# A four-stage block (two attentions, two feed-forward parts): x and weights split into f16 halves in SBUF and transposed by DMA in place of TensorE

## The reference, cut to what matters

```python
x = x + tanh(g_xattn[0]) * L0_xattn(layernorm(x), ctx, Wq, Wg, bg, Wkv, Wo)     # 16 heads, linear attention, sigmoid gate
x = x + tanh(g_ffn[0])   * L0_ffn(layernorm(x), proj1, b1, proj2, b2)           # 512 -> 2048 -> 512, gelu
x = x + tanh(g_xattn[1]) * L1_xattn(layernorm(x), ctx, mask)                    # softmax over 64 memory tokens
x = x + tanh(g_ffn[1])   * L1_ffn(layernorm(x), gate_w, gate_up, down, ...)     # router, 8 experts of 192, silu(gate) * up
```

## Time and profile before

| | |
|---|---|
| median of 3 runs | 1939.32 us (1937.81 to 1941.26) |
| the profiled execution's own time | 1941.13 us |
| its span, first to last instruction | 1939.3 us |
| TensorE (PE) busy | 1900.6 us, 98% |
| weight loads (PEld) | 962.7 us, 50%, beside PE |
| VectorE (DVE) | 1035.4 us, 53% |
| ScalarE (ACT) | 559.7 us, 29% |
| GpSimd (POOL) | 280.7 us, 14% |
| mean granted TensorE clock | 0.994 |
| DMA | 86.99 MB, mean 45 GB/s |

### The profile page before, as it was taken

The page is one execution under the profiler, slowest core; times in us unless marked ns, Lnnn a source line. Parts: engine busy times, 40 slices in busy tenths (PEclk is TensorE's granted clock), DMA queues, the critical chain, the costliest instruction groups (busy, mean ns, idle before and its releaser), DMA issues.

```text
span 1939.3 us, 25583 instructions
## 1 busy us (share of the span) xinstructions
PE 1900.6 (98%) x10102; PEld 962.7 (50%) x10102; DVE 1035.4 (53%) x2260; ACT 559.7 (29%) x873; POOL 280.7 (14%) x277
## 2 busy tenths in 40 slices
PE   6999998999999999999999999999999999999999
PEld 4556555644444444444444444444544444444444
DVE  7688866764545453443535545554555555545422
ACT  3145423422222221112212233232222333333321
POOL 3023211111102010101100011111111111111111
PEclk9999998999999999999999999999999999999999
DMA  6013322220101111110101020101010101000000
GB/s 218 12 42 124 106 89 82 87 98 17 44 28 60 28 64 50 56 55 22 62 1 55 1 71 1 50 1 50 1 50 1 50 1 45 5 11 13 1 22 22
DMA packets 56041, 86.99 MB, mean 45 GB/s; under 512 B 9042, under 2 KB 17362, under 8 KB 55922
## 3 DMA queue, kind: packets, MB, share of 16 engines
q1 hardware_dynamic: 55922, 85.36, 13.8%
HBM read 60.17 MB, written 25.17 MB: 44 GB/s over the span
## 4 chain that ended last, share of the span: by engine, by line
PE 86%; issue 8%; DVE 3%; POOL 1%; DMA 1%; ACT 1%; POOLq 0%; SPq 0%; DVEq 0%
PE bank L835 44%; PE bank L939 16%; PE bank L1033 10%; PE bank L844 5%; PE bank L919 4%; PE bank L885 1%; PE bank L904 1%; POOL arena L802 1%; PE bank L1020 1%; PE bank L968 1%; PE bank L995 0%; DMA x_after_ffn<-arena 0%; PE bank L984 0%; PE bank L983 0%; DMA arena<-x_after_attention 0%
## 5 line engine op out<-in xcount | busy, mean ns | idle before, releaser
L835 PE MATMUL bank<-arena 128*128 128x512 f16 x4608 | 1043.4, 380 | 3.1 <-DVE arena L1286 2.3
L835 PEld LDWEIGHTS bank<-arena 128*128 128x128 f16 x4608 | 451.0, 98 | 522.7 <-issue 5.5
L939 PE MATMUL bank<-arena 128*128 128x512 f16 x1536 | 352.1, 379 | 1.2 <-DVE arena L1469 1.2
L1033 PE MATMUL bank<-arena 128*128 128x512 f16 x1152 | 264.3, 379 | 0.9 <-POOL arena L802 0.9
L1621 DVE SCALAR_TENSOR_TENSOR arena<-bank,arena 128x512 f32<-128x512 f32 x96 | 72.0, 750 | 332.1 <-PE bank L835 332.1
L939 PEld LDWEIGHTS bank<-arena 128*128 128x128 f16 x1536 | 150.1, 98 | 173.9 <-DVE arena L1469 1.7
L1467 DVE TENSOR_SCALAR arena<-arena 128x512 f16<-128x512 f32 x128 | 69.4, 543 | 305.4 <-ACT arena L1134 305.2
L1134 ACT ACTIVATE arena<-bank,arena 128x512 f32<-128x512 f32 x128 | 99.6, 778 | 457.3 <-PE bank L835 454.3
L802 POOL TENSOR_TENSOR arena<-arena 128x512 f16<-128x512 f32 x96 | 111.1, 1157 | 628.7 <-ACT arena L1171 628.7
L844 PE MATMUL bank<-arena 128*128 128x128 f32 x1012 | 150.1, 279 | 26.4 <-DVE arena L1234 14.1
L1033 PEld LDWEIGHTS bank<-arena 128*128 128x128 f16 x1152 | 112.1, 98 | 128.3 <-POOL arena L802 1.4
(11 more groups left out here) (173 smaller groups left out, 1221.9 us busy)
## 6 DMA issues: line engine op xcount, KB each, us to landing
arena<-in_L_ffn_proj SPq DMA_DIRECT2D x48, 256.0 KB, 2.9
x_after_attention<-arena SPq DMA_DIRECT2D x8, 1024.0 KB, 4.7
arena<-x_after_attention SPq DMA_DIRECT2D x8, 1024.0 KB, 5.6
x_after_ffn<-arena SPq DMA_DIRECT2D x8, 1024.0 KB, 4.5
arena<-x_after_ffn SPq DMA_DIRECT2D x8, 1024.0 KB, 6.2
arena<-in_x SPq DMA_DIRECT2D x7, 1024.0 KB, 5.4
out<-arena SPq DMA_DIRECT2D x7, 1024.0 KB, 4.2
arena<-in_L_ffn_down_proj SPq DMA_DIRECT2D x48, 96.0 KB, 2.0
```

The lines of the kernel that those rows point to most:

```text
L835: m = e.matmul(bank[b][:, :], wT[l][:, c, tile * P:(tile + 1) * P], y[h][:, c, :], start=n == 0, stop=n == NPASS - 1)
L939: m = e.matmul(bank[t][:, :], hv[h][:, 0, t * P:(t + 1) * P], w2T[l][:, j, :], start=j == 0 and i == 0, stop=j == NH - 1 and i == 2)
L1033: m = e.matmul(bank[t][:, :], hv[h][:, 0, t * P:(t + 1) * P], dnT[l][:, j, :], start=j == 0 and i == 0, stop=j == NR - 1 and i == 2)
```

## The change: what it does

Both turns leave TensorE and PSUM. ACT now makes the `hi` half where the tile lies, from SBUF (`split` for x, `wsplit` for weights), the `lo` half is made beside it (for x by POOL, for weights by DVE), and one DMA transpose, issued by SP, moves the 128 x 1024 f16 tile (256 KB) of both halves into eight 128x128 blocks of the destination. POOL's scaling of row weights is gone: the scale is applied in the splits. x has four split buffers (`ysp`), weights three (`wsp`). In the attention stage all four x tiles are turned in the norm's last step; its `norm` steps stand earlier in the list. At the start, the small loads and those of Wkv and ctx are placed behind the first x turns. `w2T` and `dnT` are laid out by fours to suit the blocks.

```diff
 def second(w):
         add("wlo", w)
+        add("wturn", w)
 def weights(upto=N_D):
-                add("wturn", w, banks=1)
+                add("wsplit", w)
 def step(t):
-            if t > 1:
-                add("turn", i, t - 2, banks=1)
             if t < NT:
                 add("norm", i, t)
+            if 0 < t <= NT:
+                add("split", i, t - 1)
+            if i[0] != "A" and t > 1:
+                add("turn", i, t - 2)
+            elif i[0] == "A" and t == NT + 1:
+                for k in range(NT):
+                    add("turn", i, k)
...
-        if i == 3:
+        if i == NT + 2:
             add("small")
-        if i == 4:
             add("kvload")
...
-            if 0 < b < NB and j >= 2:
+            if 0 < b < NB:
                 norms.pop(0)()
...
-                if b > 0 and j == 0:
+                if j == 0:
                     for _ in range(2):
                         norms.pop(0)()
...
+    wsp = [at(215 + 2 * i, D, F16) for i in range(3)]
+    ysp = [at(207 + 2 * i, D, F16) for i in range(NT)]
...
 def sync_program(e):
             elif kind == "wload":
-                        w.wait_ge(w_turned, nth["wturn", k - 4])
+                        w.wait_ge(w_lo, nth["wlo", k - 4])
+            elif kind == "turn":
+                _, i, t = step
+                w.wait_ge(y_lo, nth["split", i, t])
+                y_free(w, i)
+                e.dma_start(y_both(i)[:, :, t * P:(t + 1) * P], ysp[t], transpose=True).then_inc(y_in[t], 16)
+            elif kind == "wturn":
+                _, name, t = GROUPS[step[1]]
+                i = (nth[step] - 1) % len(wsp)
+                src = wsp[i][0:NE, :] if name == "gw" else wsp[i]
+                w.wait_ge(w_lo, nth[step])
+                e.dma_start(w_dst(name, t), src, transpose=True).then_inc(w_turned[i], 16)
...
  def pool_program(e):
+            elif kind == "split":
+                t = step[2]
+                w.wait_ge(y_hi, n)
+                e.tensor_tensor(ysp[t][:, D:2 * D], yn_s[(n - 1) % 2], ysp[t][:, 0:D], ALU.subtract).then_inc(y_lo)
-            elif kind == "wmax" and GROUPS[step[1]][0] == "row":
-                e.tensor_scalar(stg[k % 4], stg[k % 4], wrec[:, c], W_TOP, ALU.mult, ALU.mult).then_inc(w_scaled)
...
  def scalar_program(e):
+            elif kind == "split":
+                e.activation(ysp[t][:, 0:D], yn_s[(n - 1) % 2], ACT.Copy).then_inc(y_hi)
+            elif kind == "wsplit":
+                i, m = (n - 1) % len(wsp), (n - 1) // len(wsp)
+                if m:
+                    w.wait_ge(w_turned[i], 16 * m)
+                e.activation(wsp[i][:, 0:D], stg[k % 4], ACT.Copy, scale=scale).then_inc(w_hi)
...
  def vector_program(e):
             elif kind == "wlo":
+                e.scalar_tensor_tensor(out=wsp[i][:, D:2 * D], in0=stg[k % 4],
+                                       scalar=wrec[:, c] if how == "row" else sc["s" + name], in1=wsp[i][:, 0:D],
+                                       op0=ALU.mult, op1=ALU.subtract).then_inc(w_lo)
...
  def tensor_program(e):
             if kind == "q":
-                w.wait_ge(y_lo, y_rank(("A", b)))
-                w.wait_ge(w_lo, n_lo["q"])
+                y_ready(w, ("A", b))
+                w_ready(w, "q")
```

More of the change, by code:

```diff
@@ L405, in build @@
     tg = at(120, NC * TOK).rearrange("p (c n) -> p c n", c=NC)
-    dnT = pair(112, NR, D)
+    dnT = in_fours(112, NR, D)
     xsl = [at(k, NT * D).rearrange("p (t n) -> p t n", t=NT) for k in (136, 144, 128, 24, 40)]
     yT = [pair(152, NC, TOK), pair(160, NC, TOK)]
+    yT_both = [at(152 + 8 * i, NC * TOK, F16).rearrange("p (k n) -> p k n", k=2 * NC) for i in range(2)]
     aT = yT[1]
@@ L461, in build @@
     domt = small(NG, I32)
-    gwT = [small(NC * NE // 2, F16).rearrange("p (c s) -> p c s", c=NC) for _ in range(2)]
+    gw_both = small(NC * NE, F16).rearrange("p (a s) -> p a s", a=2 * NC)
+    gwT = [gw_both[:, NC * i:NC * (i + 1), :] for i in range(2)]
     bank = [stack.enter_context(nc.psum_tensor(f"bank{i}", [P, 512], F32)) for i in range(8)]
@@ L527, in w_nth, with w_ready, n_rows @@
         return nth[kind, w]
-    n_lo = {}
-    for i, (how, name, t) in enumerate(GROUPS):
-        if how != "max" and t == SIZE[name] - 1:
-            n_lo[name] = nth["wlo", i]
+    n_turned = {name: nth["wturn", i] for i, (how, name, t) in enumerate(GROUPS) if how != "max" and t == SIZE[name] - 1}
+    def w_ready(w, name):
+        for i in range(len(wsp)):
+            w.wait_ge(w_turned[i], 16 * ((n_turned[name] - 1 - i) // len(wsp) + 1))
+    def n_rows(k):
+        return sum(g[0] == "row" for g in GROUPS[:k + 1])
     def freed(step, i):
         kind, n = step[0], nth[step]
-        if kind == "turn":
-            return y_lo, n
-        if kind == "wturn":
-            return w_lo, n
         if kind == "q":
@@ L634, in build, with y_ready @@
         w_landed[w] = landed[w % 4]
-    def y_rank(i):
-        return nth["turn", i, NT - 1]
+    def y_ready(w, i):
+        for t in range(NT):
+            w.wait_ge(y_in[t], 16 * nth["rs", i])
     def bcast(v):
@@ L848, in tensor_program @@
             kind, n = step[0], nth[step]
-            if kind == "turn":
-                w.wait_ge(const, C_ID)
-                w.wait_ge(yn_ok, n)
-                turn4(step, yn_s[(n - 1) % 2], y_turned)
-            elif kind == "wturn":
-                k = step[1]
-                how, name, t = GROUPS[k]
-                w.wait_ge(const, C_ID)
-                if how == "row":
-                    w.wait_ge(w_scaled, sum(g[0] == "row" for g in GROUPS[:k + 1]))
-                else:
-                    w.wait_ge(w_in[k % 4], w_landed[k])
-                turn4(step, stg[k % 4], w_turned)
-            elif kind == "q":
+            if kind == "q":
                 _, b, j = step
-                w.wait_ge(y_lo, y_rank(("A", b)))
-                w.wait_ge(w_lo, n_lo["q"])
+                y_ready(w, ("A", b))
+                w_ready(w, "q")
                 project(step, wqT, j, yT[0], q_mm)
@@ L1007, in tensor_program @@
                 _, b, j = step
-                w.wait_ge(w_lo, n_lo["gate"])
-                w.wait_ge(y_lo, y_rank(("M", b)))
+                w_ready(w, "gate")
+                y_ready(w, ("M", b))
                 project(step, gateT, j, yT[b % 2], ge_mm)
@@ L1054, in y_free, with y_both @@
             w.wait_ge(sc_mm, b + 1)
-    def y_of(i):
-        return yT[0] if i[0] == "A" else yT[i[1] % 2]
+    def y_both(i):
+        return yT_both[0 if i[0] == "A" else i[1] % 2]
     def scalar_program(e):
@@ L1064, in scalar_program @@
             kind, n = step[0], nth[step]
-            if kind == "turn":
+            if kind == "split":
                 _, i, t = step
-                w.wait_ge(y_turned, n)
-                y_free(w, i)
-                e.activation(y_of(i)[0][:, :, t * P:(t + 1) * P], block4(bank_of[step, 0]), ACT.Copy).then_inc(y_hi)
+                w.wait_ge(yn_ok, n)
+                if nth["rs", i] > 1:
+                    w.wait_ge(y_in[t], 16 * (nth["rs", i] - 1))
+                e.activation(ysp[t][:, 0:D], yn_s[(n - 1) % 2], ACT.Copy).then_inc(y_hi)
             elif kind == "consts":
@@ L1072, in scalar_program @@
                 e.activation(tanhg, gains, ACT.Tanh).then_inc(tanh_ok)
-            elif kind == "wturn":
+            elif kind == "wsplit":
                 k = step[1]
                 how, name, t = GROUPS[k]
+                c = slice(COL0[name] + t, COL0[name] + t + 1)
+                if how == "row":
+                    w.wait_ge(w_rec, n_rows(k))
+                    scale = wrec[:, c]
+                else:
+                    w.wait_ge(w_in[k % 4], w_landed[k])
+                    w.wait_ge(scale_of[name], 1)
+                    scale = sc["s" + name]
+                i, m = (n - 1) % len(wsp), (n - 1) // len(wsp)
+                if m:
+                    w.wait_ge(w_turned[i], 16 * m)
+                e.activation(wsp[i][:, 0:D], stg[k % 4], ACT.Copy, scale=scale).then_inc(w_hi)
                 if name in SQUARED:
-                    c = slice(COL0[name] + t, COL0[name] + t + 1)
-                    w.wait_ge(w_scaled, sum(g[0] == "row" for g in GROUPS[:k + 1]))
                     if n_sq:
```

102 lines of the change are left out of this document (42 added, 60 removed).

## The result

| | before | after |
|---|---|---|
| median | 1938.72 us (1937.81 to 1941.26) | 1962.52 us (1961.70 to 1965.40) |
| span of the profiled execution | 1939.3 us | 1963.6 us |
| first `up` of the first feed-forward part begins | 410.54 us | 489.20 us |
| from there to the end | 1528.8 us | 1474.4 us |

The medians are of four runs each. The ratio is 1.0124 [1.0108, 1.0140]. The forecast was 1866 us and "faster". The time fell inside the wide range given (1846 to 2020), but the sign was wrong, and 1962.5 us is far from the forecast's own range of 1848 to 1885. The first attention became 78.7 us longer, and all that comes behind it 54.4 us shorter.

A forecast was written before the change was run, and what follows sets the result against it. TensorE was taken as the bound (98% busy, 86% of the chain of waits). Sum: 1941.1 - 86.1 + 10 + 2.3 - 4 + 3 = 1866.3 us, stated as 1866; own range 1848 to 1885, 8-in-10 range 1846 to 2020.

The forecast's parts named there:

- What goes: TensorE's stream: 197 transpose turns of x and weights behind 42 us leave, at 0.437 us each, saving 86.1 us.
- T: SP's queue: distance between successive 256 KB DMA transposes, taken as 2 us; break-even just above 4.
- Rival 2: Attention stage: transposes above 4 us make SP's queue or DMA rings the new bound, launch slower; chance 0.31.
- Rival 1: Between gate and q in attention: transposes of 2.6 to 4 us stall and eat the gain, 1885 to 1935 us; chance 0.14.
- the norm is earlier in the list now: At the 286 us all-reduce: out matmuls can run in TensorE's gap; 4 us gained, ends 0 and 8.
- hidden, until T = 2.6: Batches 2 to 7, last gate to next q: four transposes need 10.6 us within 13.06, so no stall.
- 25 us of 37: SP's queue late in attention: 11 transposes and 7 loads take 25 us of a 37 us batch, hidden until T about 3.
- The other two signs: Signs of a wrong forecast: scores or router waits over 1 us; ACT stands before a weight split for lack of a buffer.
- The start: Before the first q: eight transposes must land, q at 32.1 us, 11.7 later; net loss 10 us.
- for which 2.3 were booked: Batch 1, last gate to first q: four transposes need 10.6 us, so 2.6 us of turns are not gained; loss 2.3 us.
- The 286 us gap: TensorE stands from 287.2 to 297.27 behind an all-reduce; out matmuls were to fill it, gaining 4 us.
- POOL beside DVE: First attention: DVE's SBUF-to-SBUF forms stretch while POOL works beside them; 3 us lost, ends 0 and 10.

The follow-up runs named there:

- e11: The changed kernel (after) with each 128 x 1024 transpose of x issued as two of 128 x 512; 1995.68 us, ratio 1.0289.
- e3: The kernel before, transposes on TensorE, with only the norm's statistics moved earlier in the list; 1961.75 us, ratio 1.0115.
- e6: The changed kernel (after) with x of the attention stage stored and loaded in four tiles of 256 KB; 1933.61 us, ratio 0.9965.
- e5: The changed kernel (after) with an attention batch's four x transposes put right behind the last gate, ahead of the weight step; 1947.43 us, ratio 1.0038.
- e9: e7 with the subtraction for x's lo half moved from POOL to DVE, one place behind the split; 1925.44 us, ratio 0.9929.
- e7: The changed kernel (after) with the edits of e5 and e6 together; 1920.94 us, ratio 0.9908.
- e13: The changed kernel (after) with the first attention's x turned on TensorE in the old list places, and x stored and loaded in 256 KB tiles; 1883.34 us, ratio 0.9710.
- e10: e7 with batch 0's x tiles turned one by one and its q waiting only for its own weight tile; 1919.25 us, ratio 0.9895.

## Why the prediction was wrong, step by step

**What goes: right.** Behind the first stage lie 129 of the 197 turns; at 0.437 us they are worth 56.4 us, and 54.4 came. From one `scores` to the next the experts' batch took 103.69 us before (1357.80 to 1461.49) and takes 100.18 now (1297.63 to 1397.81): 3.5 us less, as said. The profile of after has 176 transposes left on TensorE, as said.

**T: right in kind, and kinder than assumed.** 1.34 us against 2. The 1.3 us worked out from the 20 ns of a small packet was the number, but by luck. Between before and after the packets under 512 bytes grow from 9042 to 228,978, that is 1052 for each of 209 transposes, near the 1024 assumed. But in e11 128 more transposes add only 4096 such packets to those of after, so each there has about half as many, and it holds SP as long: the packets do not set the price. The page "VectorE: DVE Perf Modes" of the Trainium skill (the three transpose paths) has 1309 ns for one 128x128 block by DMA; the runs agree if that is read as a price for each issue, and disagree with the reading as eight blocks in turn (10.5 us). Rival 2's sign came true, but its mechanism (T above 4) did not. Rival 1 named the right place, four transposes in a row between `gate` and `q`, with stalls from there, but tied it to a T of 2.6 to 4 us.

**The step that failed: "the norm is earlier in the list now", booked as free and even as a gain, and with it the term "hidden, until T = 2.6" for batches 2 to 7, booked at nothing.** The prediction used a gapless timeline of before for batches 2 to 7 and took the halves as ready at the last `gate`. It priced the transposes in SP's queue by their sum (25 us of 37), and never asked what SP *waits* for ahead of them. Two things were missed. The statistics in the first place of a batch need an x whose load is issued only behind the store of the batch before: e3 shows 22 us for that alone, e6 gives 29 us back. And a weight reload, which waits for DVE, stands ahead of the x turns: e5 gives 15 us back. That `q` would wait for x transposes in batches 2 to 7 was named in advance as a sign of failure, and the profile shows it in four of the six (5.88, 6.21, 6.44 and 3.96 us). The other two signs are there too, but small: one `router` waits 1.2 us, and ACT stands before weight splits 5.2 us in 4.

**What the idle time cost beyond itself.** In after the first group of `q` behind a wait takes 4.63 us in place of 2.75. The windows (from:to, length, busy time of PE with its instructions, PEld, DVE, ACT, POOL, granted clock, DMA share, GB/s) show why:

```profile
150.00:160.00 10.00, 9.98 (x47) 4.30 (x44) 9.45 (x32) 4.58 (x10) 1.16 (x1) 1.00 0.34 84
160.00:165.80 5.80, 0.00 (x0) 0.00 (x0) 2.69 (x8) 0.00 (x0) 0.00 (x0) 0.75 1.07 210
165.80:170.40 4.60, 4.54 (x13) 1.74 (x14) 0.00 (x0) 0.00 (x0) 0.00 (x0) 0.58 0.60 130
170.40:176.00 5.60, 5.60 (x32) 3.02 (x31) 1.95 (x3) 1.98 (x3) 1.27 (x1) 1.00 0.48 174
```

TensorE stood 5.88 us, its mean granted clock is 0.58, near the lower of its two levels (1.2 of 2.4 GHz), for 4.6 us behind that, and full again from 170.4. In e5, with a wait of 1.77 us in the same place, the group took its 2.75 us. So the wait of 5.88 us is paid with 1.9 us more. Over the stage from 120 to 400 us the mean clock is 0.90 in after and 0.98 in before. The prediction had no term for this.

**The start: right in size, partly by luck, and wrong in reach.** `q` began at 30.57 (forecast 32) and k and v at 54.03, 12 us later than before; the 10 us booked are those. Two errors cancel in the 32: by its own rule a T of 1.34 gives about 27, but the first transpose was issued at 15.31 and not at 13.5, and weight loads and a wait stand between the eight. But 8.8 us more are lost by batch 1's first `q` (121.54 against 100.74), for which 2.3 were booked: the wait for its own transposes (5.30 us) and one for DVE ahead of it (6.73 us).

**The 286 us gap: wrong.** A gain of 4 us was booked; in after the wait is 12.59 us where it was 9.90. It belongs to a chain through POOL around the all-reduce. The earlier norm of after did not shorten it, and neither did taking the `lo` halves off POOL (11.24 us in e9).

**POOL beside DVE: 3 us booked, not measured apart.** The line of 816 ns in the earlier trace rows takes 928 ns now, 14 us of DVE's time over its 128 instructions:

```profile
L1480 DVE SCALAR_TENSOR_TENSOR arena<-arena 128x512 f16<-128x512 f32 x128 | 118.7, 928 | 4.6
```

Part of it lies beside TensorE's work; the rest is somewhere in the last item of the account.

**The account.** The forecast for the first `up` is 410.5 - 68 x 0.437 + 10 + 2.3 - 4 + 3 = 392.1; it was 489.2, so 97 us are missing. What e5 and e6 mend together is 41.6 of them (e7). What is left between e7 and e13, 37.6 us, goes with x of this stage on DMA transposes and all that it brings (four in a row, halves on POOL, the larger start), but not with that alone: e13 also has the statistics in their old place, and in e7 they still wait 16.4 us for `in_x`. To this come the 14.0 us of 32 turns that e13 forgoes. That is 93.2; the 4 us that remain are given to nothing. How the 37.6 us divide between POOL, the row of four, the start and the rest of the early statistics is not settled: e9 moves 8 us of it and e10 none. And e13 is not free of loss in this stage: its first `up` is at 409.59, 1 us before that of the kernel before, though all the weight turns are gone. The items are differences of medians of the launch, the first `up` is of one profiled execution each, so the sum is good to a few us.

## What to carry to other kernels

Before an instruction is called hidden by its duration, look at what its queue waits for ahead of it: here the transposes' own time was over-estimated, and the largest part of the loss that was traced came from waits for others' work. A step that is moved up in an in-order list is as early as its latest input allows and blocks its engine until then; find the load that it reads, and the store that this load waits for. And where a stage has enough slack on its queues (here, all behind the first attention) an exchange of TensorE time for DMA pays almost in full (54.4 of 56.4 us), so such a change may be made stage by stage: e13 keeps the part that pays.

## What was not expected of the hardware

- A DMA transpose inside SBUF mostly holds SP for 1.23 to 1.35 us whether it moves 128 x 512 or 128 x 1024 f16 elements (e11), where most plain loads of a weight tile hold it for 0.33 to 0.6 us. Single ones held it longer (3.60 us at 53.57 in after); why is open. It lands 3.2 us behind its issue at 256 KB and 2.5 us at the mixed sizes of e11 (medians). A larger one was not tried.
- A stall of 1.77 us of TensorE left its next group at 2.75 us; one of 5.88 us made it 4.63 us (e5 and after). The same was seen behind shorter stalls close together: in e13 the first `q` group of batch 1, at 109.62, took 5.01 us behind waits of 2.88, 1.16 and 1.42 us, with a mean granted clock of 0.66 from 100 to 115 us.
